# Edge vectors of a graph layer: one load issued earlier, and eight small VectorE operations placed earlier in the schedule

## The reference

```
r     = edge_vec / |edge_vec|                      # one 3-vector per edge
sh1   = sqrt(3) * r
xs,xd = x[edge_src], x[edge_dst]                   # 8 scalars + 8 vectors per node
w     = relu(emb @ fc1_w1 / ..) @ fc1_w2 / ..      # per-edge weights of the first layer
s_t,v_t = products of (xs, xd, sh1) with w         # first tensor product
w2    = relu(emb @ fc2_w1 / ..) @ fc2_w2 / ..
scal, gates, vecs = products of (s_t, v_t, sh1) with w2
edge_out = [tanh(scal), vecs * tanh(gates)] * norm
y     = layernorm(x + segment_sum(edge_out, edge_dst))
```

## Time and profile before

| | |
|---|---|
| time, median of 3 runs | 761.84 us (761.58 to 762.68) |
| span of the profiled execution, first to last instruction | 759.7 us |
| VectorE busy | 716.8 us, 94% of the span, 1321 instructions |
| TensorE busy | 678.2 us, 89% |
| ScalarE busy | 552.6 us, 73% |
| GpSimd busy | 528.3 us, 70% |
| the chain of work that ended last | PE 57%, DVE 31%, waiting for nothing shown 4%, ACT 3% |

### The profile page before, as it was taken

One profiled execution on the slowest core, in us unless ns is written; L12 is line 12 of the kernel. 1 busy time (PEld: TensorE's weight loads), 2 busy tenths in 40 slices (PEclk: granted clock), 3 DMA queues, 4 the chain that ended last, 5 costly groups with the idle time before them and its releaser, 6 DMA issues.

```text
span 759.7 us, 20521 instructions
## 1 busy us (share of the span) xinstructions
PE 678.2 (89%) x6623; PEld 297.1 (39%) x6726; DVE 716.8 (94%) x1321; ACT 552.6 (73%) x1279; POOL 528.3 (70%) x655
## 2 busy tenths in 40 slices
PE   0788999999999999999999999999999999999963
PEld 0433444434444444444434443444444443444321
DVE  8689999999999999999999999999999999999973
ACT  3367777777777777777777777777777777777741
POOL 8778877688768877787768776887688767876100
PEclk9699999999999999999999999999999999999997
DMA  4321211111112111111112111211121111111000
GB/s 124 81 61 25 46 25 39 27 47 28 39 23 48 27 29 40 41 27 28 41 29 45 26 39 24 48 27 42 23 45 27 37 28 38 28 26 24 11 1 22
DMA packets 45180, 27.34 MB, mean 36 GB/s; under 512 B 23157, under 2 KB 43654, under 8 KB 45075
## 3 DMA queue, kind: packets, MB, share of 16 engines
q1 hardware_dynamic: 30726, 18.15, 8.9%
q0 software_dynamic: 13312, 6.84, 6.0%
q10 hardware_dynamic: 1036, 1.02, 0.5%
HBM read 21.77 MB, written 4.20 MB: 34 GB/s over the span
## 4 chain that ended last, share of the span: by engine, by line
PE 57%; DVE 31%; issue 4%; ACT 3%; DMA 0%; POOL 0%; DVEq 0%; ACTq 0%
DVE z_s L736 24%; PE ps L985 14%; PE ps L921 12%; PE ps L965 7%; PE ps L893 5%; PE ps L912 4%; PE ps L885 4%; PE ps L940 4%; DVE p_s L698 3%; PE ps L905 1%; ACT e_part L508 1%; ACT h L498 1%; PE ps L953 1%; PE ps L932 1%; PE ps L972 1%
## 5 line engine op out<-in xcount | busy, mean ns | idle before, releaser
L335 POOL DMA_INDIRECT xs<-in_xp,src_i x416 | 401.6, 965 | 114.9 <-issue 104.5
L698 DVE TENSOR_TENSOR p_s<-ps,h 128x2048 f32<-128x2048 f32 x104 | 238.2, 2290 | 7.6 <-PE ps L985 7.6
L736 DVE TENSOR_TENSOR z_s<-ps,h 128x2048 f32<-128x2048 f32 x104 | 238.3, 2291 | 3.6 <-PE ps L940 1.0
L486 ACT CAST v_s<-ps 128x512 bf16<-128x512 f32 x312 | 181.3, 581 | 37.6 <-PE ps L905 34.9
L985 PE MATMUL ps<-f,w_f 32*128 32x512 f32 x832 | 119.9, 643 | 29.1 <-DVE z_s L736 25.8
L921 PE MATMUL ps<-z_s,w_z 128*32 128x512 f32 x832 | 111.7, 609 | 3.6 <-DVE z_s L736 2.4
L905 PE MATMUL ps<-p_s,sum_m 128*32 128x512 f32 x832 | 111.7, 609 | 0.3
L455 ACT COPY f<-ps 128x512 f32<-128x512 f32 x104 | 60.8, 585 | 41.8 <-PE ps L893 41.8
L449 ACT COPY oht<-ps 42x512 bf16<-42x512 bf16 x104 | 60.1, 578 | 35.3 <-PE ps L885 35.3
L377 POOL TENSOR_TENSOR along<-fe,r 128x192 f32<-128x192 f32 x104 | 54.5, 524 | 45.0 <-ACT fe L467 44.0
L492 ACT ACTIVATE h<-ps 128x512 f32<-128x512 f32 x104 | 62.1, 597 | 32.2 <-PE ps L972 31.5
(11 more groups left out here) (115 smaller groups left out, 878.2 us busy)
## 6 DMA issues: line engine op xcount, KB each, us to landing
emb<-e_dram SPq DMA_DIRECT2D x309, 30.0 KB
xs<-in_xp,src_i POOLq DMA_INDIRECT x416
e_dram<-e_part SPq DMA_DIRECT2D x7, 360.0 KB
e_in<-in_emb SPq DMA_DIRECT2D x8, 240.0 KB, 2.8
window<-x_dram SPq DMA_DIRECT2D x104, 7.9 KB
x_dram<-eo_all SPq DMA_DIRECT2D x3, 195.3 KB
eo_all<-in_vec_t SPq DMA_DIRECT2D x1, 528.0 KB, 3.7
xt_n<-in_xt SPq DMA_DIRECT2D x1, 400.0 KB
```

The costliest lines, as they stand in the source:

```text
L335: nc.gpsimd.indirect_dma_start(xs_r[n][:, t, :], None, xp, bass.IndirectOffsetOnAxis(src_i[:, m * T + t:m * T + t + 1], axis=0)).then_inc( ...
L486: nc.scalar.copy(v_s[:], v_ps).then_inc(v_step, 1)
L698: nc.vector.tensor_tensor(p_s[:], ps[:, 0:4, :], h1_r[m % 2][:].unsqueeze(1).to_broadcast([128, 4, BE]), ALU.mult).then_inc(p_done, 1)
L736: nc.vector.tensor_tensor(z_s[:], ps[:, 0:4, :], h2_r[k % 3][:].unsqueeze(1).to_broadcast([128, 4, BE]), ALU.mult).then_inc(z_done, 1)
```

## The change

The load of the vectors of tiles 64 to 415 is issued by SP right behind the weights (some 23 us earlier), with a semaphore of its own. The eight VectorE operations stand at steps -2, -2, 0, 0, 0, 1, 1, 1 instead of 0, 1, 3, 4, 5, 6, 7, 8. The square root on ScalarE stands in step -1, between `part_of_v` 1 and `copy_sources`, instead of the end of step 2. What is computed stays the same.

```diff
+        vect_rest_loaded = sem("vect_rest_loaded")
...
             sp.dma_start(w_z[:].rearrange("p n c -> p (n c)"), w2b).then_inc(weights_loaded, 16)
+            sp.dma_start(vt[:, TA:TILES, :], vec_t[:, TA:TILES, :]).then_inc(vect_rest_loaded, 16)
             sp.wait_ge(zeroed, 1)
...
             load_window(3)
-            sp.dma_start(vt[:, TA:TILES, :], vec_t[:, TA:TILES, :]).then_inc(vect_loaded, 16)
             sp.dma_start(src_i[:, TA:TILES], src_t[:, TA:TILES]).then_inc(src_loaded, 16)
...
                 if real(i):
                     part_of_v(i, 1)
+                if i == -1:
+                    act.wait_ge(n2_ready, 2)
+                    nc.scalar.activation(nrm_t[:, TA:TILES], n2_t[:, TA:TILES], ACT.Sqrt).then_inc(norm_ready, 1)
                 if real(i + 3) and i < 2:
                     copy_sources(i + 3)
...
                 later_emb(i)
-                if i == 2:
-                    act.wait_ge(n2_ready, 2)
-                    nc.scalar.activation(nrm_t[:, TA:TILES], n2_t[:, TA:TILES], ACT.Sqrt).then_inc(norm_ready, 1)
...
                 if step == 0:
-                    dve.wait_ge(vect_loaded, 16 if first == 0 else 32)
+                    dve.wait_ge(vect_loaded if first == 0 else vect_rest_loaded, 16)
...
-                for step, at_step in enumerate((0, 1, 3, 4, 5, 6, 7, 8)):
+                for step, at_step in enumerate((-2, -2, 0, 0, 0, 1, 1, 1)):
```

## The result

The changed kernel takes **759.97 us** (median of 22 runs, 758.24 to 762.72) against 761.88 us before (22 runs, 761.30 to 763.48). The ratio is 0.9971, with a 95% interval from 0.9963 to 0.9980: faster by 1.5 to 2.8 us. The forecast was 759.8.

A forecast was written before the change was run, and what follows sets the result against it. Bound: a closed loop of z_s on DVE and PE's work, 6.63 us a step, with little air on DVE. Terms -3.51 + 0.62 + 0.5 + 0.35 = -2.04 us, giving 759.8 us; range 758.3 to 761.5.

The forecast's parts named there:

- the three signs: Wrong if xp's cast starts after 9.1, steps 4 to 9 are not 6.63 long, or L607 slows POOL's gathers.
- Steps 3 to 9: Loop: removing six direction operations from DVE in steps 3 to 8 gives back at most 3.51 us.
- uncovered table load: Steps 3 and 4 on ACT: Tanh's table load loses its cover, L985 late by about +0.5 us, bounds 0 to 1.3.
- the cast of step 4: Cast of embeddings on ACT, no longer covered by DVE's extra work: +0.35 us, bounds 0 to 0.37.
- rival 3: Table switch costs more, or ACT's lateness goes round the loop in several steps: sum -0.8, 761.1 us; chance 14%.
- The fill: Step -2: L607 and L609, 2.5 us, fit DVE's 4.90 us idle time; cost 0, bounds for the fill 0 to -0.1.
- Step 0 and its cap: L612, L614, L616 replace L607: DVE at 39.44 ties with PE's 39.48, cost 0, capping any gain of the fill.
- Step 1: L618, L620, L621 replace L609 on DVE: +0.94 us, of which +0.62 is left at step 3.
- 1 (ACT catches up): Table load and cast hide in unseen idle pieces of ACT: -2.9, 758.9 us; chance 16%.
- 2 (DVE is the bound): DVE's removed work counts in full: -4.6, 757.2 us; chance 4%.
- Rival 4: Early 528 KB load holds up xp and the first loads, L529 up to 4.3 us later: +1.4, 763.2 us; chance 6%.
- Rival 5: DVE reaches step -2 before the vectors, or chained operations cost much more: near 761.5 us; chance 4%.

The follow-up runs named there:

- tanh_early: The changed kernel with one idle one-column Tanh on ScalarE behind the square root in step -1, loading its table in the fill; 759.87 us.
- all_early: The changed kernel with squares on ScalarE, sum, square root and reciprocal in step -2, the other five operations in step 0, Tanh table loaded early; 759.43 us.
- act_square: The changed kernel with the squares of the vectors on ScalarE before 19 us instead of on VectorE in step -2; 759.99 us.
- no_rest: The kernel before without the directions of tiles 64 to 415, their load and square root, set to 1 by a memset; 758.10 us, ratio 0.9959.
- load_only: The kernel before with only the early load, the square root and eight VectorE operations at their old steps; 761.53 us, ratio 1.0010.

## Why the prediction was right, point by point

**The size was right, from terms that were partly off.** Forecast for step 10: -2.04. Measured: -1.59 in one profile and -1.87 in the other, against one profile of the kernel before; -1.9 in the medians. That the median came within 0.2 us of the forecast is in part luck. Two of the three signs that I named for being wrong came true (xp's cast later than 9.1, L607 slowing POOL's gathers), the terms ahead of step 3 were 0.6 too low, and the last stretch, which moves an execution by 1.6, was in no term.

**Steps 3 to 9** were the gain: 49.92 us before, 104.23 - 57.13 = 47.10 now. The forecast was 46.41 + 0.5 + 0.35 = 47.26. Every step that I called undisturbed took 6.63. The uncovered table load cost 0.34 (forecast 0.5), and tanh_early shows that it was the table load; the cast of step 4 cost 0.35, as foreseen from the earlier trace rows. In all_early the step without the table load takes 6.88 for another reason, so the 0.34 holds for this schedule only. Once nothing covers it, Tanh still follows its load without a gap, as in the earlier trace rows, so rival 3 falls, and with it for this switch the 2.66 us of the Trainium skill, ScalarE: Activation LUTs, section "What ACT_TABLE_LOAD costs": 1.28 us for the load is what the trace has, and only 0.34 of it reached z_s of step 5.

**The fill was called free, and cost 0.3 to 0.5** (z1 in the two profiles). "2.5 us fit, cost 0" held for DVE's idle time. What failed is that I let nobody else pay: I listed L607 slowing POOL's gathers among the things that would prove me wrong, and gave it no price. act_square shows it: the gather that began 0.52 us into the product took 1.55 us instead of 0.95, and POOL releases sum_along, so it came straight onto the path. Where the same product stood before, at 35.94, a gather began 0.04 ahead of it and took 0.95, so the trace of before gave no warning.

**Step 0 and its cap were right**: p_s of block 1 without idle, on DVE's heels, 0.04 a handover. The cap worked both ways: the tie I forecast at 39.44 became 39.96 by the 0.6 of POOL.

**Step 1** was forecast at +0.94 and cost +1.08: L622 took 1.33, one_hot 0.39. At step 3 the sum is +1.23 instead of +0.62: 0.47 from the fill, 0.14 from here. DVE's wait for POOL in step 2 shrank to 0.71 and hid nothing of it from the loop. These 0.6 us are the largest term that was mis-sized.

**The bound was named for the wrong reason.** "The groups say why: L985 waits for DVE" failed. The 25.8 us are holes where 103 records of L912 are missing; PE is busy without a break. The number taken from it, 6.63 us a step, was read from starts of z_s and stood. A price worked out from that idle time would have been wrong.

**Rivals.** 1 (ACT catches up) is out: 0.34 and 0.35 are there. 2 (DVE is the bound) is out: no_rest gains 3.1, not 5. Rival 4 had its mechanism right and not its end: xp's cast slipped by 1.27, past the 0.88 of air that I gave it and past the 9.1 that I had named as the line, and the fill did not move, because DVE's next subtraction then began ahead of POOL's and took 0.99 instead of 1.94. I had read the Trainium skill, DMA: Bandwidth & Descriptors, section "Queues, rings and completion order", as if xp could not be overtaken at all. It says that descriptors are consumed in ring order on each DMA engine, and in the same sentence that a later one may finish its write before an earlier one. The trace shows that being first in the queue did not keep xp's landing where it was. The 528 KB themselves took 8.3 us from issue to landing, where I had taken 4.3, and were still there long before 26. load_only puts the price in the median at nothing that can be told. Rival 5 is out: L608 begins at 26.10 without a wait, and a handover costs 0.03 to 0.04.

**The end of the execution** was in no term of mine. "From step 10 on nothing is changed" is right for the instructions, and z_s keeps its lead to 0.04 us over 94 steps; but the last stretch takes 27.1 us in the profile of before and 28.7 in both of the changed kernel, by when the clock comes back; in the profiles of the other kernels without idle matmuls there it takes 27.0 to 28.8. Why it came back sooner in some was not found. The range was wide enough for it, but not because of it.

## What to carry to other kernels

Work that is moved into an engine's idle time is not free for its neighbours: ask who runs beside it there, and whether that engine releases somebody who waits. Read what moved work can give from the starts of one recurring instruction over the affected steps (here 49.92 against 7 x 6.63), not from its durations; and before an idle time in a table of groups is believed, count the records of the instruction ahead of it. When a change is worth 2 us in 760, the fill and the last steps of a profile can hide or double it; compare the lead at a fixed instruction in the middle.

## What the runs showed of the hardware that was not expected

- A product of two SBUF operands on VectorE and GpSimd's work disturb each other, in both directions: a gather's issue took 1.55 us instead of 0.95 where it began 0.50 to 0.53 us into a 128x1056 product, and mostly stayed at 0.94 to 0.95 where the two began within 0.04 us of each other (once it took 2.03); a 125x800 subtraction on VectorE took 1.94 us where it began behind one on GpSimd, and 0.99 where it began ahead of it; a 128x64 product took 0.75 instead of 0.21 beside GpSimd's of 1.15. In the cases with a clear order the one that began later paid; no run varied this order alone.
- In waits of TensorE of 1.68 to 2.37 us (before p_s of block 1 in all_early, before the last z_s in the kernel before) the granted clock fell from 2.4 to 1.2 GHz. At the end of the kernel before it was low from 735.0 to 738.4 and again from 741.9 to 745.2, at the end of the changed one from 732.8 to 746.4. Fourteen idle matmuls in two such waits took 3.0 us off the last stretch beside one profile of the kernel before, and 4.6 beside the changed kernel's.
